# A second low-rank product form, half the key transfers, new engine orders and 43 identity products on the tensor engine

## The reference

```
x = LN(x + attention0(x))   16 heads of 8, low-rank q and k, causal
x = LN(x + ffn0(x))         silu(x W1) * (x W2), two 512x512 layers with gelu, W3
x = LN(x + attention1(x))   16 heads of 8, softmax without scale, then / sqrt(128)
x = LN(x + ffn1(x))
ffn1: e     = argmax(x gate_W + gate_b)                   one of 8 experts a token
      inter = relu(x wi + wi_b + (x lora_A[e]) lora_B[e])  rank 4
      out   = inter wo + wo_b
```

## Time and profile before

| | |
|---|---|
| median of three runs | 875.84 us (875.03 to 881.42) |
| profiled execution: time, span | 876.6 us, 874.5 us |
| mean granted clock of TensorE | 0.958 |
| busy: PE, PEld | 823.0 us (94%), 626.7 us (72%) |
| busy: DVE, ACT, POOL | 611.2 us (70%), 402.6 us (46%), 190.5 us (22%) |
| chain that ended last | PE 75%, DVE 7%, ACT 5%, DMA 4%, SP's queue 4% |

### The profile page before, as it was taken

How to read it: one execution, slowest core, us unless ns; L and a number is a source line. 1 busy time by engine, 2 the same in 40 slices (tenths; PEclk the granted TensorE clock), 3 DMA queues, 4 the chain that set the end, 5 groups by cost and what they waited for, 6 DMA issues and landing times.

```text
span 874.5 us, 21713 instructions
## 1 busy us (share of the span) xinstructions
PE 823.0 (94%) x8690; PEld 626.7 (72%) x8690; DVE 611.2 (70%) x1715; ACT 402.6 (46%) x823; POOL 190.5 (22%) x398
## 2 busy tenths in 40 slices
PE   8679999999989999999999999999999899999885
PEld 6457776777767687877778786877778677777554
DVE  3574685968668587877768786848847784847554
ACT  1323536273643736273554628182463627371441
POOL 4332421130302122131313113040211314010001
PEclk9789899999999999999999999999889999999779
DMA  6522222201330221213240302313020400111200
GB/s 217 203 85 74 85 87 76 75 27 61 119 121 4 87 73 37 82 56 106 68 153 21 128 32 65 104 50 112 4 92 15 141 4 27 55 36 46 87 9 13
DMA packets 43468, 64.19 MB, mean 73 GB/s; under 512 B 6088, under 2 KB 34088, under 8 KB 42984
## 3 DMA queue, kind: packets, MB, share of 16 engines
q1 hardware_dynamic: 41688, 57.93, 20.2%
q10 hardware_dynamic: 1680, 4.87, 1.6%
HBM read 43.41 MB, written 18.35 MB: 71 GB/s over the span
## 4 chain that ended last, share of the span: by engine, by line
PE 75%; DVE 7%; ACT 5%; DMA 4%; SPq 4%; issue 3%; POOL 2%; POOLq 0%; DVEq 0%; ACTq 0%
PE banks L1116 25%; PE banks L1065 10%; PE banks L1098 6%; PE banks L1172 6%; PE banks L976 5%; PE banks L1032 5%; ACT prob L618 3%; DVE top L741 3%; PE banks L943 3%; PE banks L1145 3%; DMA krow<-scratch 2%; PE banks L1077 2%; SPq L480 2%; PE banks L952 2%; PE banks L1047 2%
## 5 line engine op out<-in xcount | busy, mean ns | idle before, releaser
L741 DVE TENSOR_REDUCE top<-banks 128x3 f32<-128x384 f32 (+1 forms) x512 | 290.0, 613 | 72.7 <-PE banks L983 50.4
L618 ACT ACTIVATE prob<-banks 128x384 f32<-128x384 f32 (+1 forms) x512 | 242.0, 560 | 91.6 <-PE banks L1040 43.1
L632 ACT ACTIVATE hid<-banks 128x512 f32<-128x512 f32 x64 | 38.1, 597 | 237.0 <-PE banks L1116 237.0
L555 POOL TENSOR_TENSOR ln_rstd<-ln_var,minus_half 128x2 f32<-128x2 f32 x64 | 44.5, 701 | 439.7 <-DVE ln_var L820 439.4
L1065 PE MATMUL banks<-prob,v 128*32 128x256 f32 (+1 forms) x2048 | 122.0, 373 | 7.7 <-POOL prob L562 4.6
L1116 PE MATMUL banks<-glu,wh 128*128 128x256 f32 x512 | 120.3, 389 | 0.0
L1116 PE MATMUL banks<-hid,wh 128*128 128x256 f32 x512 | 119.3, 387 | 0.1
L1116 PEld LDWEIGHTS banks<-glu,wh 128*128 128x128 f32 x512 | 96.7, 194 | 15.6 <-issue 1.0
L1116 PEld LDWEIGHTS banks<-hid,wh 128*128 128x128 f32 x512 | 96.1, 193 | 13.9 <-DVE top L741 0.4
L1065 PEld LDWEIGHTS banks<-prob,v 128*32 128x32 f32 x2048 | 59.3, 113 | 53.0 <-issue 11.5
L976 PE MATMUL banks<-krow,qrow 32*128 32x256 f32 (+1 forms) x992 | 76.9, 336 | 14.8 <-DMA krow<-scratch 10.8
(11 more groups left out here) (110 smaller groups left out, 1027.1 us busy)
## 6 DMA issues: line engine op xcount, KB each, us to landing
scratch<-split SPq DMA_DIRECT2D x124, 128.0 KB, 2.2
qrow<-scratch SPq DMA_DIRECT2D x31, 512.0 KB, 3.6
krow<-scratch SPq DMA_DIRECT2D x124, 128.0 KB, 3.2
xt<-in_xt SPq DMA_DIRECT2D x16, 128.0 KB, 2.6
wh<-in_wh ACTq DMA_DIRECT2D x2, 1024.0 KB, 7.7
out<-xout SPq DMA_DIRECT2D x16, 128.0 KB, 2.1
x<-in_x SPq DMA_DIRECT2D x15, 128.0 KB, 3.0
prob<-in_qk_a SPq DMA_DIRECT2D x2, 512.0 KB, 4.9
```

Source lines behind the costliest of these rows:

```text
L555: nc.gpsimd.tensor_tensor(ln_rstd[s][:], ln_var[s][:], minus_half[:], ALU.pow).then_inc(rstd[s], 1)
L618: nc.scalar.activation(prob[s][:, j % 2, g, 0:wide], banks[:, b, 0:wide], ACT.Exp, scale=1.0 / float(np.sqrt(np.float32(HD))) if s == A0 e ...
L632: nc.scalar.activation(hid[layer][:, 2 * m:2 * m + 2, :].rearrange("p m t -> p (m t)"), banks[:, g, :], ACT.Gelu).then_inc(gelued, 1)
L741: nc.vector.tensor_reduce(out=top[s][:, :, h], in_=banks[:, b, 0:blocks * wide].rearrange("p (q k) -> p q k", q=blocks), axis=AX, op=ALU.m ...
```

## The change

The low-rank product goes over to f32r in parts. `route` writes the picked values as a rounded part and a rest, each twice, into all 128 columns of `low`; `wlb` holds four copies of lora_B, two rounded and two of the rest (made by DVE once, ahead of route 0). One product over 128 rows then gives all four pairs of parts. Relu starts pair by pair. The keys are fetched by two transfers of 64 partitions each, which repeat their source. All five orders and the bank table are new; PE's order has 43 letters `b`, each two products of the identity with itself into a bank. The count of every other letter is the same on each engine.

```diff
 SEQUENCE = {
     "pe": (
-        "dcaaadeaffgahfhfahahcaiagjrrffadfhhsasafshhgsaitfcjufyarfhharfzdcahhAsAgsAfisfaAsBfhhtCafduCDhCjyDharCri"
...
-        "fcMtfjNBhfOhfCuyCrDChhDCrizDDAsAsAEsAsFBPMtNCjOCuDyCrDCrDDsAsAEsAsAFtPBuzMyNCCDODCAAAADPCzBDCECCDFDCMDDN"
-        "EOFMPNOP"
+        "adcabbabbadebbfbfgahfhaabbfbahbhgbbbaicbffajhfrfhdrahhscasgaisasftfjdfhuchayzrfrahhsigAsaAsaAsAftBfjbarC"
...
+        "FiDADasAszAgsAMsfjBtrfNruChhfEyCOfsChDhDAsiCsjAsFArrtPADDsuzBMysCEsCsADtCDANCubAyFbbADDbbbBMzbEONbbbACbA"
+        "CbADCDAPFCBOzMDDCPNCEDCDCFOMDDNPEObbFbbMPbNbbObbbbP"
     ),
...
     "act": (
-        "xddxffffffffffffffffxjrrfffffffffffdfssffffssffffujfffyfrffffrffffdssffffffffssffffCCCCfffudCCfCCCjCyCCC"
...
+        "dxdffffffffffffxffffxfffffffjfffffrffffdrssssffffffjffdfffuyfrffffrssssfffffjfffrCCCCruffyffCCCCfffCdCfC"
...
-        wlb = sb("wlb", [P, HID])
+        wlb = sb("wlb", [P, HID], F32R)
...
-        low = sb("low", [P, TILES, P])
-        lowt = sb("lowt", [P, TOK])
+        low = sb("low", [P, TILES, PARTS, PARTS * ER])
+        low_parts = sb("low_parts", [P, TILES, PARTS, ER])
+        chosen = sb("chosen", [P, TILES, ER])
+        lowt = sb("lowt", [P, TOK], F32R)
...
-                for i in range(PARTS):
-                    for k in range(PARTS):
-                        sp.dma_start(krow[s][n % DEEP[s]][PARTS * i + k::PARTS * PARTS].bitcast(F32).rearrange("p j t -> p (j t)"),
-                                     scratch[s][n % 2][1, :, k]).then_inc(there, DMA)
+                for k in range(PARTS):
+                    sp.dma_start(krow[s][n % DEEP[s]][k::PARTS].bitcast(F32).rearrange("p j t -> p (j t)"),
+                                 scratch[s][n % 2][1, :, k].unsqueeze(1).to_broadcast([GROUP * HD, PARTS, GROUPS * TOK])).then_inc(there, DMA)
...
+                if is_first(n):
+                    dve.wait_ge(weights, NWEIGHTS)
+                    nc.vector.tensor_copy(wlb[:], lbraw).then_inc(lb_parts, 1)
+                    dve.wait_ge(lb_parts, 1)
+                    at = slice(PARTS * ER, P)
+                    nc.vector.tensor_tensor(wlb[at], lbraw[at], wlb[at].bitcast(F32), ALU.subtract).then_inc(lb_parts, 1)
...
+                nc.vector.tensor_copy(low_parts[:, :, 0].bitcast(F32R), src[:, :, EXPERTS:]).then_inc(routed, 1)
...
+                nc.vector.tensor_tensor(low_parts[:, :, 1], src[:, :, EXPERTS:], low_parts[:, :, 0], ALU.subtract).then_inc(routed, 1)
...
+                for k in range(PARTS):
+                    done = nc.vector.tensor_tensor(low[:, :, k].rearrange("p t (i c) -> p t i c", i=PARTS), low_parts[:],
+                                                   chosen[:].unsqueeze(2).to_broadcast([P, TILES, PARTS, ER]), ALU.mult)
...
-                for i in range(2):
-                    for pair, g in enumerate((ga, gb)):
-                        m, tile = 2 * pair + i, slice(pair * ER, (pair + 1) * ER)
-                        done = nc.tensor.matmul(banks[:, g, i * TOK:(i + 1) * TOK], wlb[tile, m * P:(m + 1) * P], lowt[tile],
+                if is_first(n):
+                    pe.wait_ge(lb_parts, PARTS)
+                for pair, g in enumerate((ga, gb)):
+                    for i in range(2):
+                        m = 2 * pair + i
+                        done = nc.tensor.matmul(banks[:, g, i * TOK:(i + 1) * TOK], wlb[:, m * P:(m + 1) * P], lowt[:],
                                                 start=False, stop=True, skip_group_check=True)
-                done.then_inc(exp_full, 1)
+                    done.then_inc(exp_full, 1)
```

More of the change, by code:

```diff
@@ L419, in build @@
         NPARKED = 2 * PARTS * DMA
-        NSPREAD = (1 + PARTS * PARTS) * DMA
+        NSPREAD = (1 + PARTS) * DMA
         NMAX = PARTS * DMA
@@ L423, in build @@
         NWEIGHTS2 = 2 * DMA
-        NWEIGHTS = 8 * DMA
+        NWEIGHTS = (6 + PARTS * PARTS) * DMA
         NSCALED = 5
+        ROUTED = 9
         block = ctx.enter_context(nc.Block())
@@ L529, in _ @@
                     nc.gpsimd.memset(top[s][:].rearrange("p q h -> p (q h)"), 0.0)
-            nc.gpsimd.memset(low[:].rearrange("p t c -> p (t c)"), 0.0).then_inc(blank, 1)
-            pool.wait_ge(blank, 3)
+            pool.wait_ge(blank, 2)
             nc.gpsimd.memset(ones[:].bitcast(F32), 1.0).then_inc(ones_made, 1)
@@ L590, in late @@
                 else:
+                    act.wait_ge(folded, 2)
                     for dst, name in ((wq[A1][:], "qk_w1"), (wv[A1][:], "v_w1"), (wo[A1][:], "o_w1"), (wi[:], "wi"), (wgl[:], "gl"),
-                                      (wlb[0:ER], "lb"), (wlb[ER:2 * ER], "lb"), (wout[:], "wo")):
+                                      *((lbraw[i * ER:(i + 1) * ER], "lb") for i in range(PARTS * PARTS)), (wout[:], "wo")):
                         act.dma_start(dst, d_in[name]).then_inc(weights, DMA)
@@ L642, in expert @@
                     act.wait_ge(scaled_w, NSCALED)
[L643 removed]
                 for pair, g in enumerate((ga, gb)):
+                    act.wait_ge(exp_full, PAIRS * n + pair + 1)
                     for i in range(2):
@@ new lines, in route @@
+                step(2, nc.vector.tensor_tensor(logit[:], src[:, :, 0:EXPERTS], row("gate_b").unsqueeze(1).to_broadcast(wide), ALU.add))
+                nc.vector.tensor_tensor(low_parts[:, :, 1], src[:, :, EXPERTS:], low_parts[:, :, 0], ALU.subtract).then_inc(routed, 1)
+                step(4, nc.vector.tensor_reduce(out=best[:], in_=logit[:], axis=AX, op=ALU.max))
+                step(5, nc.vector.tensor_tensor(pick[:], logit[:], best[:].unsqueeze(2).to_broadcast(wide), ALU.is_ge))
+                step(6, nc.vector.tensor_tensor(pick[:], pick[:], ranks[:].unsqueeze(1).to_broadcast(wide), ALU.mult))
@@ new lines, in route @@
+                step(7, nc.vector.tensor_reduce(out=first[:], in_=pick[:], axis=AX, op=ALU.min))
+                wider = [P, TILES, EXPERTS, LORA]
+                step(8, nc.vector.tensor_tensor(chosen[:].rearrange("p t (e r) -> p t e r", r=LORA), pick[:].unsqueeze(3).to_broadcast(wider),
+                                                first[:].unsqueeze(2).unsqueeze(3).to_broadcast(wider), ALU.is_equal))
+                for k in range(PARTS):
+                    done = nc.vector.tensor_tensor(low[:, :, k].rearrange("p t (i c) -> p t i c", i=PARTS), low_parts[:],
+                                                   chosen[:].unsqueeze(2).to_broadcast([P, TILES, PARTS, ER]), ALU.mult)
@@ L1129, in route @@
                 done.then_inc(route_full, 1)
-                last.used(g, routed, 7 * n + 7)
+                last.used(g, routed, ROUTED * n + ROUTED)
             def lora(s, n, g):
-                pe.wait_ge(routed, 7 * n + 7)
+                pe.wait_ge(routed, ROUTED * n + ROUTED)
                 last.wait(pe, g)
                 for t in range(TILES):
-                    done = nc.tensor.transpose(banks[:, g, t * P:(t + 1) * P], low[:, t, :], ident[:])
+                    done = nc.tensor.transpose(banks[:, g, t * P:(t + 1) * P], low[:, t].rearrange("p j c -> p (j c)"), ident[:])
                 done.then_inc(lora_full, 1)
```

95 lines of the change are left out of this document (43 added, 52 removed).

## The result

The changed kernel takes 833.67 us (median of four runs, 829.21 to 836.12) against 878.63 us for the kernel before beside it (875.03 to 881.78). The ratio is 0.9484, with a 95% interval of [0.9422, 0.9546]. The profiled execution took 836.12 us, its span 834.4 us, the mean granted clock 0.981.

A forecast was written before the change was run, and what follows sets the result against it. PE's own work was taken to bound 100 to 800 us, with looser ends. 876.6 - 13.9 - 4.4 - 5 - 2 = 851.3, then -2.1 for the tail, gave 849 us, range 838 to 870.

The forecast's parts named there:

- moved behind the last `t`: PE steps the new order leaves until after the last F0 `down` step, which then comes 13.9 us sooner.
- product, 11 chunks: Low-rank product in f32r before the last `t`: 0.40 us saved a chunk, 4.4 us in all.
- head: Start of the kernel: a shorter key wait before chunk 1 and warm steps keeping the clock, 5 us saved.
- middle: Stretch between head and last `t`: 2 us saved, for the stall at 252 us and its clock; 0 to -14 possible.
- stretch behind the last `t`: The tail: 13.9 us of moved work added, less 2.0 for experts, 8 for filled gaps, 6 for clock: -2.1.
- The key transfers: Two of four key issues go: 1.2 us off each of 31 trips, up to 0.4 given back in landing.
- rival 2: Key trip of A1 becomes a wait in each chunk if an issue exceeds 0.8 us: 874 us, chance 0.12.
- a wait below 3 us: Sign that the forecast holds: PE's wait for `krow` near chunk 1 falls below 3 us.
- the 75 that I had set as a sign of being wrong: Sign against the forecast: the stretch after the last `t` longer than 75 us; about 67 us was expected.
- Rival 1: Identity products do not keep the clock and tail gaps do not take the moved work: 863 us, chance 0.18.
- Rival 3: Warm steps stand in the way as plain work, 19 us and 10 more in the tail: 892 us, chance 0.06.
- faster than 840: Case beyond the forecast in which the middle's clock comes back too: below 840 us, chance 0.03.

The follow-up runs named there:

- n2: Kernel before with the new orders and bank table, identity steps issuing nothing, product and key transfers left old: 839.73 us, ratio 0.9536.
- n3: Kernel after with the orders and bank table of the kernel before, keeping the new product and two key transfers: 876.42 us, ratio 0.9942.
- n1_no_warm: Kernel after with its 43 identity steps issuing nothing: 829.3 us, ratio 0.9416 against the kernel before.
- e13_old_spaced: Kernel before with 39 value steps of the middle moved one letter later in PE's order alone: 916.89 us, ratio 1.0353.

## Why the prediction was right in sign and too small in size

The balance in us of span, predicted and measured on the profiled executions:

| term | predicted | measured |
|---|---|---|
| moved behind the last `t` | -13.9 | -13.9 (letters counted, not measured) |
| product, 11 chunks | -4.4 | -4.4 (11 x 0.40) |
| head | -5 | +1.5 (the remainder) |
| middle | -2 | -28.3 (beyond own cost) |
| stretch behind the last `t` | -2.1 | +5.0 |
| sum | -27.4 | -40.1 (874.5 to 834.4) |

**The product: right.** From an expert step's first record to the next step's first is 2.39 us, against 2.79 before (336.82 - 333.47 - 0.56): 0.40 us less, the term as taken. Before, the next step has to be counted in, as it starts while the four small products still run: from start to start alone it is 2.26 us.

```profile
312.92 1.99 PE L1157 MATMUL banks<-xt,wi 128*128 128x256 f32 x8
314.56 0.82 PE L1165 MATMUL banks<-lowt,wlb 128*128 128x256 f32 x4
315.31 0.51 PE L1044 MATMUL banks<-qrow,krow 32*128 32x256 f32 x8
```

There are 64 such records and not 128, and their starts stand 0.31, 0.12 and 0.12 us apart in a step. The rule of the Trainium skill that spoke against this part (TensorEngine Tiling (Array Packing), Overview: a contraction of at most 32 can be packed up to four times) didn't decide here, where a packing by two was given up and the sum did not come out higher. VectorE's longer `route` stays hidden in the new orders, but for waits of 1.2 and 0.3 us on `low`. In the old ones it doesn't (4.5 us in six waits, above): that the cost hides was right for the new orders only.

**The key transfers: right in the issue, short in the landing.** Two issues in 1.25 us, 0.6 each, as said, so rival 2 (an issue over 0.8 us) had no ground, and no wait per chunk came up. PE's waits for `krow` past 100 us did grow, from 3 of 3.2 us in all to 6 of 5.9. But doubling the bytes of a transfer costs 1.1 us of landing, where 0.4 was the bound and 0.3 the Trainium skill's formula gives (DMA: Bandwidth & Descriptors, section Anatomy of one DMA, the two cost components, fitted on transfers that GpSimd issues). It nearly eats the 1.2 us saved. The measurement decides: about 1 us in all, which can't be told from none.

**The head: wrong.** PE's wait for `krow` ahead of chunk 1 did go from 6.3 to 2.7 us, but since PE had more work before it, not since the keys came sooner: that pass1 starts at 34.5 us as against 34.7. So the sign that I had set, a wait below 3 us, came true by luck. I named the collision of chunk 1's fetch with 2 MB of `wh` and saw that it goes; I didn't look at the first loads, which the same order moved behind the first split, onto the parking. The run with the loads first starts that pass1 3.9 us sooner than the kernel after. Chunk 2's fetch, which I named as a possible loser, is a loser too (a 3.8 us wait, 17.1 us at half speed from 51.6 us on).

**The middle: the step that failed.** I read the waits there as "short and of many kinds", PE as "98% busy", and took 2 us. It was 28.3. Two readings were wrong. First, the busy share was taken for PE's own work ("so there the time is PE's own work"), though at that share the starts of the steps stand up to 50.6 us further apart than their own costs (besides what lies at half speed), and 28.3 us less so in the new orders. Second, my bound for the middle (0 to -14) held the clock alone, half of 28 us, and nothing for waits inside busy time. The fall at 626.8 us stands behind bunched short steps, and the new orders have no such fall before 750 us. The runs put it on the orders (n2 against n3), not on the identity products, which gave the middle nothing. Within the orders, about half of the difference goes with the length of the score steps' readers (13.5 of 29.3 us); the kept clock makes up to 13 us, part of the same difference. What makes the rest is not settled: it is neither ACT's table loads nor VectorE's maxima by themselves, and single value steps moved in PE's list alone can't settle it, since both directions were slower.

**The tail: mis-sized.** It went to 75.3 us where I had 68, past the 75 that I had set as a sign of being wrong. I had 8 us of moved work filling gaps and 6 from the clock. Without the identity steps the time at rest behind the last `t` went from 16.4 to 13.1 us (73.70 - 60.57), so 3.3 us were filled; the clock went from 0.84 to 0.90, which is 22.5 - 14.7 = 7.8 us less at half speed, 3.9 back. Then 70.2 + 13.9 - 2.0 - 3.3 - 3.9 = 74.9, against 73.7 measured. So little of the moved work fits into the gaps at the end. The identity steps add 1.6 to the tail and give it 0.92.

**The rivals.** Rival 1 was half right: the 43 identity products are not what holds the middle's clock, and the tail's gaps took little of the moved work; but the clock held without them. Rival 3 (43 x 0.45 us in the way) is refuted, and so is its 892 us: against n1_no_warm the 43 steps cost some 4 us, the doubled ones some 6, with what the clock gave back taken off. The case that came true, faster than 840, had 0.03 in my forecast, and its reason there was the clock alone.

## What to carry to other kernels

On an engine that shows 98% busy, measure the distance between the starts of successive steps against the step's own cost before calling the stretch bound by it: here overlapping records hid tens of microseconds. Judge an order of steps only with the orders of all engines that it works with; moving single steps of one list cost 0.8 to 1.0 us each here, in either direction. When a load changes its place in a queue, list every transfer that is under way at its new place, not only at the old.

## What the hardware did that I had not expected

The granted clock fell to the lower level behind stretches in which PE's records leave small gaps only, made of short steps with waits between their products (626.8 us before, behind slices of 3.63 and 3.74 us busy in 4; 492 us in e13_old_spaced). In the kernel after a fetch of keys of 256 KB landed in 4.3 us and one of queries of 512 KB in 3.8, before one of keys of 128 KB in 3.2; the first two both repeat their source, so neither size nor the repeat alone orders them. And 42 table loads of 1.28 us each on ACT cost nothing that can be measured (829.3 us with them, 827.53 without).
